# Attention and convolution: score products issued in twos, maxima and convolutions regrouped on even steps

## The reference

```
# layer 0: attention over the pixels
q = Wq x ;  k = Wk x ;  v = Wv x              # 32, 32 and 256 channels
attn = softmax(q^T k / sqrt(32))              # 4096 x 4096 per image
out  = gamma * Wo (v attn^T) + x
# layer 1, on 8x8 patches
low  = 2x2 means ;  high = patch - upsampled(low)
low  = prelu(bn(mag_w low + mag_b))
high = prelu(bn(phase_w [high, high rolled by one row] + phase_b))   # first 256 channels
out  = upsampled(low) + high
```

## Time and profile before

| | |
|---|---|
| median of 3 runs | 2368.03 us (2366.93 to 2368.57) |
| time of the profiled execution | 2367.34 us |
| its span, first to last instruction | 2365.5 us |
| PE busy | 2292.9 us, 97% |
| DVE busy | 1782.5 us, 75% |
| ACT busy | 1369.4 us, 58% |
| POOL busy | 720.5 us, 30% |
| mean granted PE clock | 0.986 |

### The profile page before, as it was taken

One profiled execution on the slowest core, in us unless ns is written; L12 is line 12 of the kernel. 1 busy time (PEld: TensorE's weight loads), 2 busy tenths in 40 slices (PEclk: granted clock), 3 DMA queues, 4 the chain that ended last, 5 costly groups with the idle time before them and its releaser, 6 DMA issues.

```text
span 2365.5 us, 48520 instructions
## 1 busy us (share of the span) xinstructions
PE 2292.9 (97%) x16885; PEld 1843.7 (78%) x16885; DVE 1782.5 (75%) x2838; ACT 1369.4 (58%) x2547; POOL 720.5 (30%) x891
## 2 busy tenths in 40 slices
PE   5799999999989999999999999999999999999997
PEld 4587888887878887888877888888887777777786
DVE  6777787777777777887767877777887777778764
ACT  3365665565655656665546665656665555555564
POOL 3232332233232232332232332232332323133222
PEclk8899999999999999999999999999999999999998
DMA  4100111000110001111100000000000000000000
GB/s 166 56 29 30 40 40 40 31 21 28 40 41 32 31 27 31 40 40 32 35 22 24 31 31 31 21 10 31 31 31 22 22 12 9 21 21 21 21 18 19
DMA packets 42119, 75.50 MB, mean 32 GB/s; under 512 B 4864, under 2 KB 6144, under 8 KB 42080
## 3 DMA queue, kind: packets, MB, share of 16 engines
q1 hardware_dynamic: 42080, 75.00, 9.8%
HBM read 55.59 MB, written 19.40 MB: 32 GB/s over the span
## 4 chain that ended last, share of the span: by engine, by line
PE 91%; issue 3%; DVE 2%; POOL 1%; ACT 1%; DMA 0%; SPq 0%; DVEq 0%; ACTq 0%; POOLq 0%
PE O L521 19%; PE O L523 18%; PE O L522 18%; PE M L374 14%; PE M L411 10%; PE S L482 10%; PE M L392 1%; ACT p L641 1%; DVE pl L897 1%; PE M L417 1%; DMA uh<-in_x 0%; PE O L374 0%; DVE on L892 0%; POOL z L1051 0%; ACT ph L638 0%
## 5 line engine op out<-in xcount | busy, mean ns | idle before, releaser
L521 PE MATMUL O<-uh,ph 128*128 128x257 f16 x4096 | 1136.3, 277 | 2.3 <-DVE pl L897 1.9
L523 PE MATMUL O<-uh,pl 128*128 128x257 f16 x4096 | 1122.8, 274 | 0.0
L522 PE MATMUL O<-ul,ph 128*128 128x256 f16 x4096 | 1119.9, 273 | 0.0
L638 ACT ACTIVATE ph<-S 128x512 f16<-128x512 f32 x1024 | 612.6, 598 | 705.5 <-PE S L482 704.9
L805 DVE TENSOR_REDUCE pmax<-M 128x1 f32<-128x512 f32 (+1 forms) x1024 | 679.8, 686 | 329.2 <-PE M L411 317.4
L897 DVE TENSOR_TENSOR pl<-p,ph 128x512 f16<-128x512 f32 x1024 | 782.2, 765 | 136.6 <-ACT p L641 131.3
L641 ACT ACTIVATE p<-S 128x512 f32<-128x512 f32 x1024 | 609.5, 595 | 0.8
L521 PEld LDWEIGHTS O<-uh,ph 128*128 128x128 f16 x4096 | 401.0, 98 | 263.4 <-issue 142.3
L482 PE MATMUL S<-qcur,kst 128*128 128x512 f32 x1024 | 486.2, 479 | 21.6 <-ACT p L641 16.8
L523 PEld LDWEIGHTS O<-uh,pl 128*128 128x128 f16 x4096 | 402.0, 98 | 51.4
L522 PEld LDWEIGHTS O<-ul,ph 128*128 128x128 f16 x4096 | 405.1, 99 | 39.0
(11 more groups left out here) (147 smaller groups left out, 1697.6 us busy)
## 6 DMA issues: line engine op xcount, KB each, us to landing
xr<-in_x SPq DMA_DIRECT2D x37, 512.0 KB, 3.7
out_y<-z SPq DMA_DIRECT2D x32, 512.0 KB, 2.8
xb<-in_x SPq DMA_DIRECT2D x25, 512.0 KB, 3.6
xs<-in_x SPq DMA_DIRECT2D x21, 512.0 KB, 3.7
qraw<-q_scratch SPq DMA_DIRECT2D x99, 64.0 KB, 1.9
ul<-in_x SPq DMA_DIRECT2D x4, 512.0 KB, 7.6
uh<-in_x SPq DMA_DIRECT2D x4, 512.0 KB, 8.3
q_scratch<-qsave SPq DMA_DIRECT2D x32, 64.0 KB, 1.6
```

The source lines that it names most:

```text
L521: nc.tensor.matmul(O[j][:, 0:UW], ph[:, t % 4, q], uh[parity][:, t, :], start=(t == 0), stop=False)
L522: nc.tensor.matmul(O[j][:, 0:C], ph[:, t % 4, q], ul[parity][:, t, :], start=False, stop=False)
L523: ins = nc.tensor.matmul(O[j][:, 0:UW], pl[:, t % 4, q], uh[parity][:, t, :], start=False, stop=(t == MT - 1))
L638: nc.scalar.activation(ph[:, t % 4, :], S[t % 2][:, :], ACT.Exp, scale=SCALE)
```

## The change

In every step before, PE issued one tile of scores. Now it issues two in every even step `t` (tiles `t + 2` and `t + 3`) and none in the odd ones. The tables of tasks are written anew: the number of maxima of each step is given outright; `y` for both halves stands in step 6, both `low` in step 20, `high` in steps 22 and 24; the maxima stand in twos at most of their steps, with three in step 28 of `FULL`. The first maximum of `FULL` is in step 2 (before: 4), the last in step 29 (before: 27), and `negmax` in step 30 (before: 29). In `LAST` the first are in step 2 (before: 3), and `negmax` in step 28 (before: 27).

```diff
-DOUBLE = (8, 10, 14, 16, 18, 22, 24, 26)
...
-FULL = Plan(steps_with_maxima({0: [("kq",), ("u", 0)], 2: [("u", 1)], 5: [("y", 0)], 6: [("y", 1)], 19: [("low", 0)],
-                               20: [("low", 1)], 21: [("high", 0)], 23: [("high", 1)]}))
+FULL = Plan(steps_with_maxima({0: [("kq",), ("u", 0)], 2: [("u", 1)], 6: [("y", 0), ("y", 1)], 20: [("low", 0), ("low", 1)],
+                               22: [("high", 0)], 24: [("high", 1)]},
+                              {2: 1, 4: 2, 5: 2, 8: 2, 9: 2, 10: 2, 12: 2, 13: 2, 14: 2, 16: 2, 17: 2, 18: 2, 22: 1, 24: 1,
+                               26: 2, 28: 3, 29: 2}))
...
+LAST = Plan(steps_with_maxima({6: [("y", 0), ("y", 1)], 20: [("low", 0, 1)], 22: [("high", 0)], 24: [("high", 1)]},
+                              {2: 2, 4: 2, 5: 2, 8: 2, 9: 2, 10: 2, 12: 2, 13: 2, 14: 2, 16: 2, 17: 2, 18: 2, 20: 1, 22: 1,
+                               24: 1, 25: 2, 26: 2, 27: 1}),
             before=(FULL, ALL - NCH))
...
+FINAL = Plan({6: [("y", 0), ("y", 1)], 20: [("low", 0), ("low", 1)], 22: [("high", 0)], 24: [("high", 1)]},
...
                 for t in range(MT):
                     if t == 0:
                         tasks(g, plan, keys_next, t)
-                    if t + LEAD < MT:
-                        scores(g, parity, t + LEAD)
+                    if t % LEAD == 0 and t + LEAD < MT:
+                        for ahead in range(LEAD):
+                            scores(g, parity, t + LEAD + ahead)
                     if t > 0:
                         tasks(g, plan, keys_next, t)
```

More of the change, by code:

```diff
@@ L64, in __init__, with steps_with_maxima @@
         self.start = kind.start + kind.uses * turns if kind else 0
-def steps_with_maxima(steps, first=4, doubled=DOUBLE):
+def steps_with_maxima(steps, counts):
     left = list(MAXIMA)
-    t = first
-    while left:
-        for _ in range(2 if t in doubled else 1):
+    for t, count in counts.items():
+        for _ in range(count):
             steps.setdefault(t, []).append(("max",) + left.pop(0))
-        t += 1
-    steps[t + 1] = [("negmax",)]
-    return steps
-FULL = Plan(steps_with_maxima({0: [("kq",), ("u", 0)], 2: [("u", 1)], 5: [("y", 0)], 6: [("y", 1)], 19: [("low", 0)],
-                               20: [("low", 1)], 21: [("high", 0)], 23: [("high", 1)]}))
-LAST = Plan(steps_with_maxima({4: [("y", 0)], 5: [("y", 1)], 19: [("low", 0, 1)], 21: [("high", 0)], 23: [("high", 1)]},
-                              first=3, doubled=(6, 8, 10, 12, 14, 16, 18, 24, 25)),
+    assert not left
+    steps[max(counts) + 1] = [("negmax",)]
+    return steps
+FULL = Plan(steps_with_maxima({0: [("kq",), ("u", 0)], 2: [("u", 1)], 6: [("y", 0), ("y", 1)], 20: [("low", 0), ("low", 1)],
[5 more added lines that the diff above has]
+                               24: 1, 25: 2, 26: 2, 27: 1}),
             before=(FULL, ALL - NCH))
-FINAL = Plan({4: [("y", 0)], 5: [("y", 1)], 19: [("low", 0)], 20: [("low", 1)], 21: [("high", 0)], 23: [("high", 1)]},
+FINAL = Plan({6: [("y", 0), ("y", 1)], 20: [("low", 0), ("low", 1)], 22: [("high", 0)], 24: [("high", 1)]},
              before=(LAST, NCH - 1))
```

## The result

The changed kernel takes 2435.89 us (median; 2434.65 to 2437.93), the kernel before in the same comparison 2368.3 us. The ratio is 1.0286, with a 95% interval of 1.0273 to 1.0300: 67.6 us slower. Forecast were 76 us more, and 2444 us.

The account below looks back on a forecast made before the run. The prediction took PE's own list of products as the bound. FULL's 65.8 us, LAST's 8.9 and FINAL's 1.0 added 75.7 us to 2367.3, giving 2443 for the profiled execution and 2444 us as median, range 2410 to 2482.

Parts of the forecast that it names:

- switches, FULL: Whole FULL turn: 9 fewer groups of float32 products, each saving 0.016 us of switching, so 0.14 us less.
- (a): Step 28 of FULL: the third maximum waits until DVE has reduced the first and freed its bank, +0.79 us.
- (b): Step 30 of FULL: negmax waits for DVE's last reductions and the negative maximum, +0.85 us.
- (c): End of FULL: the next turn's first score waits for DVE's copies after negmax's transposes, +0.25 us.
- (d): Step 2 of FULL: the second score waits for ACT's `p` of tile 3, made after the `qst` copy, +0.53 us.
- (e): Step 16: the second score waits for `p` of tile 17, behind ACT's rounding of the convolution's input, +0.26 us.
- (f): Step 13, in 16 turns with a scan: the second maximum waits for DVE to free its bank, +0.30 us.
- (g): LAST: waits in step 0, step 16 and at negmax (+0.85), 0.62 regained at the end; 1.27 us a turn.
- two rivals that lived on dear switches: Every float32 group: 0.32 us lost per switch, 2354 us, chance 0.04; or 0.16 per group's drain, 2401 us, chance 0.02.
- prediction's comparison with the Trainium skill: Float32 groups: lone product 379 ns against 216 in a stream would give 48 us gain; prediction said the trace disagrees.
- more contention: FULL turns: POOL stretches DVE's work, so (a), (b), (c), (f) reach their upper ends; 2485 us, chance 0.12.
- only the tail waits: FULL: ACT and DVE run ahead enough to hide (c) to (f); +40 us, 2407 us, chance 0.12.

Follow-up runs that it names:

- mended: Changed kernel with single scores in steps 0 to 3, rounding, scan, last maxima and negmax in other steps, LAST's first maxima in step 4: 2374.77 us.
- mended_single: Same tables, rounding and scan as mended, but the scores of one tile in every step: 2383.9 us.
- mended2: mended with FULL's first maximum moved from step 2 to 19, DVE's negative parts to step 25, LAST's normalising and low part of qst later: 2361.51 us.
- mended2_single: Same as mended2, but the scores of one tile in every step: 2375.36 us.
- small_pool: Changed kernel with POOL's sums at the end of a turn cut to 8 columns each, the rest left out: 2422.95 us.
- no_third: Changed kernel with only the third maximum of step 28 moved to a step of its own, 25: 2425.45 us.
- tail_spread: Changed kernel with FULL's last maxima rearranged over steps 21 to 28 and negmax in step 30, two steps after the last maxima: 2413.29 us.

## Why the prediction was right, and where its sizes were off

The sign, the range and the order of size came out of two readings that held. PE's own list set the end, and fewer switches were worth microseconds, while the new order put several products a turn ahead of what releases them. The terms, with what they measured in an ordinary FULL turn (with a scan where step 13 is concerned):

| step of the prediction | forecast us | measured us |
|---|---|---|
| switches, FULL | -0.14 | -0.25 (-0.17 to -0.26) |
| (a) third maximum, step 28 | +0.79 | +1.10 |
| (b) negmax, step 30 | +0.85 | +0.54 |
| (c) end of FULL | +0.25 | 0 |
| (d) second score, step 2 | +0.53 | +0.55 |
| (e) second score, step 16 | +0.26 | +0.28 |
| (f) step 13 | +0.30 | +0.44 |
| (g) LAST, second score of step 0 (1.37 less 0.24 for the score) | +1.13 | +1.15 |
| (g) LAST, negmax | +0.85 | +0.86 |
| (g) LAST, end | -0.62 | -0.28 |

The measured terms of FULL add up to 2.5 us in a turn with a scan, once the 0.13 us of small waits that the kernel before had in a turn are taken off; such turns are 2.4 to 2.6 us longer. That a FULL turn came out within 0.45 us of the forecast owes something to luck: the errors of (a) and (b) are of one size and cancel.

- **Switches.** Under-sized. The unstalled turn is 70.23 us in the kernel before and 69.98 in the changed one; counting smaller or only larger delays as waits moves the difference between 0.17 and 0.26. I had read 0.01 to 0.02 us for each from rows rounded to 0.01; over nine it is 0.02 to 0.03. The two rivals that lived on dear switches (0.16 and 0.32) are out: `mended` against `mended_single`, and `mended2` against `mended2_single`, give 0.04 (0.24 us for six groups), and even if the whole 13.9 us of the second pair were switches, its 199 groups would cost 0.07 each. (The 216 ns in the prediction's comparison with the Trainium skill stand in the section "Back-to-back issue gap" of "TensorE: Matmul & The Clock Gate", not in the one that it names; nothing else rests on them.)
- **(a)** The mechanism was right and the bank is the cause. The size missed DVE's low parts beside POOL, for which I had kept the upper bound 1.3; `small_pool` shows 0.82 without them.
- **(b)** Over-sized: the step that failed is the 0.70 us from the last reduction to the negative maximum, taken from the kernel before, where line 811 took 0.44 us. That stretch took 0.45 here, and the instruction 0.20 (0.17 in `small_pool`), when POOL had already gone on to its next sum (see the last section). In LAST the instruction still runs beside the same sum as before and takes 0.44, and there negmax costs 0.86, as forecast. A smaller part is the due time: a negmax without a score in front starts 1.32 and not 1.24 us after `weigh` even when nothing is late, so the 0.08 for the load were not an extra. And `no_third` shows that (a) and (b) are not independent, as the sum treated them.
- **(c)** Not there. I took 0.89 us for the copy of `qst` into `qcur` from the earlier trace rows; it takes 0.43 here, where POOL's sums end at 910.51. (By the prediction's own rule the term was 0.22 and 0.08, so 0.30.) In `tail_spread`, with the same step of negmax, the next turn's first score does wait, 0.67 us, but for another reason than the one added up: two low parts stand in front of the copy of negmax's row.
- **(d), (e)** Within 0.03 us. Both are chains on ACT alone, with nothing that the change or a neighbour could stretch.
- **(f)** 0.44, not 0.30: the two low parts in front were priced at 0.83 us each, the middle of 0.60 and 1.06; they take 1.93 us together here (865.14 on).
- **(g)** LAST's first wait, 1.13, measured 1.15; an ordinary LAST turn is 1.54 longer, not 1.27, mostly because the end gave back 0.28 us and not 0.62: the second score still waited there. The mean of 1.72 has in it the first of the seven, 2.80 longer, which waits 1.7 us in its first two steps; the sum had no such term.
- The first `weigh` of the run comes 3.0 us later, which the sum did not have. 1.0 us of it is the wait of LAST's step 0 once more: the first turn's second score stands 1.26 us behind its first (102.85 to 104.11) in every kernel that issues the two together. The other 2.0 us are no work of the change. Up to negmax's transposes ahead of the first turn both kernels issue the same products, and these transposes already start at 90.4 us where they started at 88.4; in the other profiled executions they start between 87.9 and 90.4. The profiled execution was the slowest of the six, 2.0 us above their median.
- The rival "more contention" had a slip of its own: the upper ends that it names make 4.25 us a turn and 2481 us, not 4.4 and 2485.

The rival "only the tail waits" is out, since (d) and (e) stood as forecast, and "more contention" happened at one place, not in all.

## What to carry to other kernels

A group of products that is moved together needs, for each of its members, the time of its releaser: the first of two fits where it did, the second may not. Here fewer switches were worth 0.02 to 0.04 us each, and a single new wait a turn outweighed all of them; take the waits out first, and test the regrouping alone afterwards. Of two consecutive waits that hang on the same engine, removing the first can move most of it into the next (0.7 of 1.10 us in `no_third`). And the length of a DVE instruction, read in one place, is a price for another place only if POOL does the same there.

## What was not expected of the hardware

Small DVE instructions differ by a factor of two and more with their surroundings: the addition on 128x4 elements took 0.44 us in the kernel before, 0.20 in the changed kernel, 0.53 in `tail_spread` (timeline of DVE, at the end) and 0.17 in `small_pool`; the copy into `qcur` 0.89, 0.43 and 0.61. What POOL does at that moment goes with it. Timeline of POOL in the changed kernel, end of the turn shown, where the addition of 908.56 takes 0.20:

```profile
903.67 3.69 POOL L1053 TENSOR_TENSOR z<-z,zneg 128x256 f32<-128x256 f32 x4
907.44 3.07 POOL L1059 TENSOR_TENSOR z<-z,zlow 128x256 f32<-128x256 f32 x4
```

Timeline of POOL and of DVE at the end of a LAST turn of the same kernel, where it stands beside the other sum:

```profile
2066.01 3.74 POOL L1053 TENSOR_TENSOR z<-z,zneg 128x256 f32<-128x256 f32 x4
2066.32 0.44 DVE L813 TENSOR_SCALAR nmax<-nmax 128x4 f32<-128x4 f32 x1
```

Over the whole traces of the kernel before, the changed kernel, `tail_spread` and `small_pool`: with POOL idle the addition takes 0.17 us, the copy 0.42 and the subtraction of line 899 0.67 to 0.70, each time. Beside the sum `z<-z,zneg` the addition takes 0.44 to 0.53 and the copy 0.94; beside `z<-z,zlow` the addition takes 0.20 at most and the copy 0.61 or 0.89. The maxima, which DVE reads from a bank and not from SBUF, take 0.67 to 0.69 whatever POOL does. The subtraction takes anything from 0.68 to 1.26 beside POOL: two take 1.83 us in step 28 and 1.31 where POOL's work is cut short, but the one of 906.07 takes 0.70 beside the same sum. What decides between short and long there stays open.

```profile
895.62 0.19 DVE L811 TENSOR_REDUCE nmax<-pmax 128x4 f32<-128x32 f32 x1
895.84 0.53 DVE L813 TENSOR_SCALAR nmax<-nmax 128x4 f32<-128x4 f32 x1
```
